# A transformer layer in one launch: the projections' query side and key side become steps of their own, and all steps stand in a new order

## The reference

```
x = layernorm(x + attn(x, x, x, causal))             # 16 heads of 8
x = layernorm(x + attn(x, context, context))
x = layernorm(x + moe(x))                            # 8 experts, top 2
attn: Q, K, V = q_in@wq+bq, k_in@wk+bk, v_in@wv+bv; softmax(QK^T/sqrt(8)) V @ wo + bo
moe:  softmax(x@router_w+b), the two largest, out = sum of w * (gelu(x@w1+b1)@w2+b2)
```

## Time and profile before

| | us |
|---|---|
| median of 3 runs | 478.7 (477.32 to 482.17) |
| the profiled execution | 477.56 |
| its span, first to last instruction | 475.8 |
| attention and routing (all 11 iterations) | 0 to about 353 |
| experts | about 364 to 446 |

### The profile page before, as it was taken

The page is one execution under the profiler, slowest core; times in us unless marked ns, Lnnn a source line. Parts: engine busy times, 40 slices in busy tenths (PEclk is TensorE's granted clock), DMA queues, the critical chain, the costliest instruction groups (busy, mean ns, idle before and its releaser), DMA issues.

```text
span 475.8 us, 8890 instructions
## 1 busy us (share of the span) xinstructions
PE 370.1 (78%) x2121; PEld 247.7 (52%) x2121; DVE 306.5 (64%) x1057; ACT 283.7 (60%) x657; POOL 162.5 (34%) x212
## 2 busy tenths in 40 slices
PE   4587699989989999989898998767603999999600
PEld 3234355646546555555456453353302999999600
DVE  6324555777787887788788877555372555555367
ACT  4064379679678678678679679526311555555314
POOL 7323032141431432522522532502220355455522
PEclk9769889999999999999999999975855999999955
DMA  8502132432351351350450450050782122222052
GB/s 249 155 0 45 41 71 54 122 71 47 90 135 33 82 154 23 86 162 7 101 160 3 102 155 9 23 150 12 220 247 50 46 64 64 62 61 56 19 177 88
DMA packets 39370, 41.60 MB, mean 87 GB/s; under 512 B 5018, under 2 KB 32527, under 8 KB 39320
## 3 DMA queue, kind: packets, MB, share of 16 engines
q1 hardware_dynamic: 37048, 36.79, 29.4%
q0 software_dynamic: 2272, 4.24, 2.6%
HBM read 13.66 MB, written 14.79 MB: 60 GB/s over the span
## 4 chain that ended last, share of the span: by engine, by line
PE 34%; DVE 27%; issue 12%; DVEq 7%; ACT 7%; DMA 5%; SPq 3%; POOL 3%; POOLq 0%; ACTq 0%
PE bank L539 7%; PE bank L481 4%; DVEq L990 4%; PE bank L482 4%; PE bank L526 4%; DVE ca_nm L820 3%; PE bank L550 3%; PE bank L507 3%; DVE ca_us L993 3%; PE bank L506 2%; DVE yb L1003 2%; ACT sa_qm L690 2%; SPq L367 2%; DVE sa_nm L820 2%; DMA sa_km<-sa_ku 2%
## 5 line engine op out<-in xcount | busy, mean ns | idle before, releaser
L749 ACT ACTIVATE sa_us<-bank,expert_b 128x128 f32<-128x128 f32 x156 | 44.9, 367 | 47.1 <-PE bank L621 33.0
L1068 POOL TENSOR_SCALAR_AFFINE_SELECT sa_pt<-sa_pt 128x512 f32<-128x512 f32 x64 | 39.0, 636 | 60.2 <-ACT sa_pt L698 60.0
L1100 POOL DMA_INDIRECT results<-sa_us,xs x39 | 41.5, 1064 | 51.2 <-DVE sa_us L1005 47.0
L820 DVE TENSOR_REDUCE sa_nm<-bank 128x4 f32<-128x512 f32 x64 | 41.5, 684 | 14.5 <-PE bank L507 13.9
L621 PE MATMUL bank<-xsT,ca_us 128*128 128x128 f32 x312 | 44.9, 288 | 2.5 <-DVE ca_us L993 1.6
L1091 POOL DMA_INDIRECT dispatched<-r_sent,r_row x32 | 31.8, 994 | 43.2 <-DVE r_sent L946 35.9
L690 ACT CAST sa_qm<-bank 8x512 fp32r<-8x512 f32 x64 | 36.9, 576 | 13.6 <-PE bank L514 11.9
L632 PE MATMUL bank<-ca_pt,sa_us 128*128 x312 | 43.5, 282 | 0.1
L690 ACT CAST ca_qm<-bank 8x512 fp32r<-8x512 f32 x64 | 36.8, 576 | 10.3 <-PE bank L514 9.2
L621 PEld LDWEIGHTS bank<-xsT,ca_us 128*128 128x128 f32 x312 | 39.3, 198 | 5.1 <-issue 3.5
L698 ACT ACTIVATE sa_pt<-bank 128x512 f32<-128x512 f32 x64 | 34.8, 596 | 10.0 <-PE bank L526 10.0
(11 more groups left out here) (210 smaller groups left out, 829.7 us busy)
## 6 DMA issues: line engine op xcount, KB each, us to landing
dispatched<-filler SPq DMA_DIRECT2D x17, 520.0 KB, 4.5
sa_km<-sa_ku SPq DMA_DIRECT2D x32, 128.0 KB, 2.4
sa_qm<-sa_qu SPq DMA_DIRECT2D x32, 96.0 KB
ca_qm<-ca_qu SPq DMA_DIRECT2D x32, 96.0 KB
xs<-dispatched SPq DMA_DIRECT2D x39, 65.0 KB
ca_km<-ca_ku SPq DMA_DIRECT2D x32, 77.0 KB, 2.1
sa_pt<-in_e_w SPq DMA_DIRECT2D x8, 256.0 KB, 4.8
ca_pt<-in_e_w SPq DMA_DIRECT2D x8, 256.0 KB, 5.7
```

The source lines that it names most:

```text
L749: act.activation(hid[b][:, c, :], bank[2 * b + c // 2][:, P * (c % 2):P * (c % 2) + P], ACT.Gelu, bias=b1[:, bass.ds(expert * FC + c, 1)]) ...
L820: dve.tensor_reduce(k.nm[:, u, g, :], bank[home[k, "scores", u][g % 2]][:, :].rearrange("q (j n) -> q j n", j=J)[:, :, 0:k.keys], AX.X, AL ...
L1068: pool.affine_select(out=blockg, in_=blockg, compare_op=ALU.is_ge, fill=0.0, base=0, pattern=[[0, J], [1, P]], channel_multiplier=-1).then ...
L1100: pool.indirect_dma_start(out=results, out_offset=bass.IndirectOffsetOnAxis(ap=xs[v][:, P:P + 1].bitcast(I32), axis=0), in_=ys[v], in_offs ...
```

## The change

`project` becomes `project` (query) and `project_keys`; `spread_terms` becomes `spread_terms` (query, q0 and q1) and `spread_keys` (key, k0 and k1); the semaphores `s_c_ps`, `s_hi` and `s_lo`, which counted both sides, become one for each side. CA's `turn` loses the context, which becomes `turn_context`, and SP's load of the context becomes the step `fetch`, one pair ahead. SP's four `km` DMAs stand in `spread_keys`, its four `qm` DMAs in `spread_terms`. `ORDER` and `home` are new throughout. No instruction that computes is added or removed. The core of the diff:

```diff
+            if not k.causal:
+                k.s_ct_ps, k.s_ct = sem(f"{name}_ct_ps"), sem(f"{name}_ct")
+            k.s_cq_ps, k.s_ck_ps = sem(f"{name}_cq_ps"), sem(f"{name}_ck_ps")
...
-            (SA, "spread_terms", 0, 1), (SA, "restore", 2, 0), (SA, "spread_terms", 1, 1), (SA, "restore", 3, 0),
...
+            (SA, "spread_keys", 1, 1), (SA, "values", 0, 1), (CA, "fetch", 0, 1), (SA, "turn_heads", 1, 0),
...
             def turn(k, p, u):
 
-                if after_pair(p):
-                    sp.wait_ge(k.s_xt_ps if k.causal else k.s_ct_ps, p)
-                if after_pair(p) or not k.causal:
+                if k.causal and after_pair(p):
+                    sp.wait_ge(k.s_xt_ps, p)
                     load_rows(k, p)
+
+            def fetch(k, p, u):
+
+                if after_pair(p):
+                    sp.wait_ge(k.s_ct_ps, p)
+                load_rows(k, p)
...
-            def spread_terms(k, p, u):
+            def spread_keys(k, p, u):
                 if u == 0:
                     return
...
+            def spread_terms(k, p, u):
+                if u == 0:
+                    return
+
+                if not after_pair(p):
+                    sp.wait_ge(k.s_zero, 2)
                 sp.wait_ge(k.s_qu, p * 2 + 2)
...
+            def turn_context(k, p, u):
+                pe.wait_ge(k.s_ld, p * 16 + 16)
+                take(home[k, "turn_context", u][0])
+                for v in range(2):
+                    ins = pe.transpose(bank[home[k, "turn_context", u][0]][:, SC * v:SC * v + SC], k.cin[:, v, :], ident[0:SC, 0:SC])
+                ins.then_inc(k.s_ct_ps, 1)
+                give(home[k, "turn_context", u][0], k.s_ct, p + 1)
...
+            def spread_terms(k, p, u):
+                pe.wait_ge(k.s_lq, p + 1)
+                spread_into(k, p, u, home[k, "spread_terms", u][0], "hq", "lq", k.hq, k.lq, k.s_rq_ps)
+                give(home[k, "spread_terms", u][0], k.s_qu, p * 2 + u + 1)
+
+            def spread_keys(k, p, u):
+                pe.wait_ge(k.s_lk, p + 1)
+                spread_into(k, p, u, home[k, "spread_keys", u][0], "hk", "lk", k.hk, k.lk, k.s_rk_ps)
+                give(home[k, "spread_keys", u][0], k.s_ku, p * 2 + u + 1)
```

More of the change, by code:

```diff
@@ L268, in build @@
         ORDER = [
[L269 to L273, removed]
@@ L279, in build @@
[L279 to L283, removed]
@@ new lines, in build @@
+            (CA, "spread_keys", 1, -1), (CA, "norm", 1, -2), (SA, "weights", 0, 0), (CA, "spread_terms", 1, -1),
+            (SA, "scores", 3, 0), (SA, "weights", 1, 0), (CA, "values", 0, -1), (RT, "route", 0, -2),
+            (RT, "gate", 0, -2), (SA, "mix", 0, 0), (SA, "shift", 1, 0), (RT, "choose", 0, -2), (SA, "mix", 1, 0),
+            (CA, "scores", 0, -1), (SA, "restore", 0, 0), (CA, "scores", 1, -1), (SA, "weights", 2, 0),
+            (RT, "fill", 0, -2), (CA, "scores", 2, -1), (SA, "turn", 0, 1), (SA, "weights", 3, 0),
@@ new lines, in build @@
+            (SA, "norm", 0, 0), (SA, "spread_terms", 1, 1), (CA, "mix", 0, -1), (CA, "weights", 1, -1),
+            (SA, "norm", 1, 0), (RT, "number", 0, -2), (CA, "weights", 2, -1), (CA, "restore", 0, -1),
+            (CA, "mix", 1, -1), (CA, "mix", 2, -1), (SA, "scores", 0, 1), (CA, "weights", 3, -1),
+            (CA, "turn_context", 0, 0), (CA, "restore", 1, -1), (SA, "scores", 1, 1), (CA, "turn", 0, 0),
+            (CA, "turn_heads", 0, -1), (CA, "mix", 3, -1), (SA, "shift", 0, 1), (CA, "restore", 2, -1),
@@ L447, in turn @@
                 give(home[k, "turn", u][0], k.s_xt, p + 1)
-                if not k.causal:
-                    pe.wait_ge(k.s_ld, p * 16 + 16)
-                    take(home[k, "turn", u][1])
-                    for v in range(2):
-                        ins = pe.transpose(bank[home[k, "turn", u][1]][:, SC * v:SC * v + SC], k.cin[:, v, :], ident[0:SC, 0:SC])
-                    ins.then_inc(k.s_ct_ps, 1)
-                    give(home[k, "turn", u][1], k.s_ct, p + 1)
+            def turn_context(k, p, u):
[5 more added lines that the diff above has]
+                give(home[k, "turn_context", u][0], k.s_ct, p + 1)
             def project(k, p, u):
@@ L950, in _ @@
             dve.wait_ge(s_setup, SETUP)
-            iterations({"gate": gate, "choose": choose, "second": second, "place": place, "number": number, "project": project, "spread_terms": spread_terms, "values": values, "scores": scores, "shift": shift, "restore": restore, "norm": norm})
+            iterations({"gate": gate, "choose": choose, "second": second, "place": place, "number": number, "project": project, "project_keys": project_keys, "spread_keys": spread_keys, "values": values, "scores": scores, "shift": shift, "restore": restore, "norm": norm})
             tables = [0]
```

136 lines of the change are left out of this document (73 added, 63 removed).

## The result

| us | before | after |
|---|---|---|
| median, 4 runs each | 479.0 (477.32 to 482.17) | 494.21 (490.0 to 495.34) |
| ratio, 95% interval | | 1.029 [1.021, 1.038] |
| profiled execution / its span | 477.56 / 475.8 | 493.3 / 491.6 |
| CA's first shift of pair 0 | 70.51 | 70.01 |
| of pair 5 | 253.24 | 268.70 |

The forecast was 477.0 with a range up to 484.5. The five intervals between the shifts of pairs 0 and 5 take 182.73 us before and 198.69 after (37.08, 40.66, 39.43, 40.67, 40.85). That is +16.0, and the profiled executions differ by 15.7. So all the loss is in the five iterations in which both the filler and a load of x are issued: +0.9, +4.1, +3.0, +4.1 and +3.9 us, 3.2 in the mean where +0.9 was forecast. The stretches outside them together give nothing where -5.45 was forecast.

The account below looks back on a forecast made before the run. No engine was taken as full; each waits a little for late inputs, most ahead of CA's shift. Terms of +4.5 and -5.45 us took 477.56 to 476.6, adjusted to 477.0; 8 in 10 runs from 467.5 to 484.5.

Parts of the forecast that it names:

- -5.45: Outside iterations 2 to 6: gains at the start and in later iterations, summing to -5.45 us.
- The load of x behind the filler: SP's queue, iterations 2 to 6: x lands 5.3 us after the first filler's issue, costing +4.5 us in all.
- Rival A: At SP's load of x: the filler holds nothing, five iterations gain 1.1 us each, 466.6 us; chance 0.28.
- I take +0.9 us an iteration: Iterations 2 to 6: late x delays CA's shift by +1.2 us, less small savings, giving +0.9 us each.
- other iterations: SP's eight DMAs: about 0.2 us less needed in iterations other than those where the late x delays the shift.
- choose and k1: Choose ahead of CA's first scores, -0.65 us an iteration; k1 directly behind k0, ku and km 0.45 us earlier.
- rival B: At SP's load of x: landing at the slow end, 6.85 us, each iteration loses 2.45, 484.4 us; chance 0.20.
- Rival C: Whole order: waits come back elsewhere; five iterations lose 0.9 us, the rest gains only 1, 481.1 us; chance 0.10.
- The context's load: SP's queue ahead of SA's qm DMAs: takes 5.9 us, covered by at least 1.8 us, so costs nothing.

Follow-up runs that it names:

- e1: Changed kernel with both filler DMAs moved back to their old place behind CA's turn; 478.77 us, ratio to the kernel before 0.993.
- e2: Changed kernel with the filler moved one place, directly behind the load of x in SP's list; 479.34 us, ratio 0.997.
- e3: Kernel before the change with only the filler moved, directly ahead of the load of x; 495.69 us, ratio 1.036.
- e5: e2 with CA's first norm ahead of the last two restores again, in bank 6; 477.9 us, ratio 0.997.
- e4: Changed kernel with ten unused matmuls added on TensorE ahead of its wait for x in iterations 2 to 6; 493.05 us, ratio 1.027.
- e11: Changed kernel with CA's norm ahead of its restores, filler still ahead of the load of x; 498.72 us, ratio 1.038.
- e13: e11 with ten unused matmuls added ahead of TensorE's wait for x, as in e4; 489.91 us, ratio 1.024.
- e10: Changed kernel with the two filler DMAs issued by ScalarE on its own queue instead of SP's; one run, 500.95 us.
- e7: Changed kernel with one filler DMA ahead of the load of x and the other behind it; 484.83 us, ratio 1.012.
- e9: Changed kernel with x loaded an iteration earlier and CA's norm ahead of its restores; 476.79 us, ratio 0.992.
- e12: e9 with GpSimd's indirect DMAs moved behind its part of CA's norm; 483.62 us, ratio 1.012.

## Why the prediction was wrong

- **The cause and the place were right.** The load of x behind the filler, TensorE's wait for `sa_xin` in five iterations and the shift behind pt all came as forecast, and moving the filler alone makes or takes away the loss (e1, e2, e3). Rival A (0.28) falls.
- **The step that failed** is "I take +0.9 us an iteration", with its working: x at 216.06, the shift near 217.5. Measured is +3.66 (40.30 against 36.64). Laid out in the same links the prediction has 1.4 from x to shift, 25.2 (204.84 - 179.66) from shift to km, 6.9 from km to load and 4.3 from load to x, in sum 37.8. The chain was right, and so was the third link (6.80). The other three were too short, by 0.4, 1.4 and 0.8 us. A further 0.3, taken off for "other iterations" and a shorter stall ahead of CA's spread, didn't come.
- **Shift to km, 1.4 us too short.** I let choose and k1 pull km forward and didn't look at what the order does between them. I had read that the restores now come ahead of the norm, and booked it as a gain in iterations 7 and 8 only. In a full iteration VectorE does CA's norm behind them, and lq, the spread and km follow: 0.8 us with the filler out of the way (e5 against e2). In the changed kernel itself the 1.4 us don't split into shares. The norm's place and the half clock each suffice to keep them (e4, e11), and with both gone the link is 25.26 (e13), which is the 25.2 of the forecast. What part VectorE's idle time next to GpSimd's indirect DMAs has in this stays open.
- **Load to x, 0.8 us too short.** The landing was taken from the median of the fillers (4.4). The 4 KB row was a weak witness for it: of its 6.8 us SP's own issue took 3.75 (4.75 to 8.50). Behind qm's traffic x is used 6.28 us after the first filler's issue (6.80 less 5.68 for km and qm, and 5.16). That is within my bounds, and above the 6.0 from which rival B was to decide. B had the sign and the mechanism, and at 484.4 it was priced 10 us too low, by the same short links.
- **TensorE's clock was in no term.** I had the rows with a clock of 1.00, and a new wait of 2 us in my own forecast, and didn't ask what the wait does to the clock. By e11 and e13 it costs up to 1.8 us an iteration; in the changed kernel, with the norm behind the restores, taking it away alone gave nothing (e4).
- **Outside, -5.45 was forecast and -0.2 came.** At the start km (issued at 13.55) is again behind a large write, the spare filler (11.27, landing 7.1 us later), and the fourth km lands later than before. The first shift still came 0.5 us earlier; the interval between the shifts of pairs 5 and 6 lost 1.2 us, where 1.1 less was forecast, 6 to 7 gained 1.3, and the rest lost 0.4. Only the start was looked into; why the terms of iterations 6 to 8 came to nothing stays open. Rival C, "a wait that goes at one step may come back at the next", describes the remainder: in e1 and e2, without the filler ahead of x, the order as a whole is worth nothing that the medians show (478.77 and 479.34 against 479.02).
- **The context's load** was covered, as forecast: SA's first weights (213.80) show no wait.

## What to carry to other kernels

Before a large transfer is moved ahead of a small load, ask whether that load lies on the loop from one iteration to the next. If it does, the delay is paid in every iteration, and a different queue didn't help here; behind the load, or with the load issued an iteration ahead, the same transfer cost nothing measurable. Where an order is changed as a whole, go through each engine's list for what now stands ahead of the loop's slowest step, and price every new wait of TensorE twice: for itself and for the clock behind it.

## What the hardware showed that I had not expected

- A load of 128 KB behind 1.04 MB of writes lands 4.8 us (median of the five) after its issue on the same queue and 6.2 with the writes on another one (e10), against 3.6 behind half of them (e7) and 2.4 with the same writes directly behind it (e2).
- In the changed kernel the waits for x of 2.1 to 3.9 us each come with a granted clock of 0.50 for 3.4 or 6.8 us, which begins in or just behind the wait. It also came behind shorter waits: 1.86 us in e9, 1.16 to 1.19 in e12. 2.33 us of useless matmuls in the wait kept the clock at 1.00 in e13's full iterations, even with 1.85 us of wait left.
- Next to GpSimd's indirect DMAs VectorE stood idle for up to 3.3 us at the restores and the norm, at times with no releaser that the profile names, and in all but the first of the full iterations at full clock of e2, e4 and e5 a restore began 21.1 to 21.3 us behind the shift. What holds them was not measured by itself.
